# A fused decoder layer on one core: the rows of the last stage turned by the DMA queue in place of TensorE

## The reference

```python
x = x + attn(layernorm(x), ...)                    # 32 query heads, int4 codes with scales
x = x + xattn(layernorm(x), ctx, ...)              # q1 @ q2, both fake-quantised to 0..255
x = x + einsum('bsi,oi->bso', layernorm(x), bw)    # bw: binarised weight, 1024 x 1024

def fake_quant(x, scale, zp):
    q = clip(round(x / scale + zp), 0, 255)
    return (q - zp) * scale
```

## Time and profile before

| | us |
|---|---|
| median of 3 runs | 1130.78 (1128.71 to 1130.89) |
| the profiled execution's own time | 1129.51 |
| its span, first to last instruction | 1127.6 |
| PE busy | 1067.3 (95%) |
| DVE busy | 933.2 (83%) |
| ACT busy | 697.0 (62%) |
| mean granted clock of TensorE | 0.99 |

### The profile page before, as it was taken

One profiled execution on the slowest core, in us unless ns is written; L12 is line 12 of the kernel. 1 busy time (PEld: TensorE's weight loads), 2 busy tenths in 40 slices (PEclk: granted clock), 3 DMA queues, 4 the chain that ended last, 5 costly groups with the idle time before them and its releaser, 6 DMA issues.

```text
span 1127.6 us, 19107 instructions
## 1 busy us (share of the span) xinstructions
PE 1067.3 (95%) x5544; PEld 524.7 (47%) x5544; DVE 933.2 (83%) x1760; ACT 697.0 (62%) x1509; POOL 693.5 (62%) x771
## 2 busy tenths in 40 slices
PE   3898998899999999999999999999999998889997
PEld 2443444344444444444444444454454454444553
DVE  6878787789888888888888889999999988867663
ACT  4356564766777777777777776666666666443320
POOL 2457445887776776776776777877787777232100
PEclk8899999999999999999999999999999999999999
DMA  9343221577777767667657756777767755501111
GB/s 353 110 150 113 66 99 38 120 157 151 167 142 158 159 138 158 159 137 158 161 134 155 163 135 143 156 153 155 165 144 148 159 120 117 180 1 38 38 37 39
DMA packets 280915, 148.66 MB, mean 132 GB/s; under 512 B 228976, under 2 KB 241520, under 8 KB 280848
## 3 DMA queue, kind: packets, MB, share of 16 engines
q1 hardware_dynamic: 273072, 134.47, 51.4%
q10 hardware_dynamic: 7776, 13.37, 4.2%
HBM read 89.07 MB, written 4.19 MB: 83 GB/s over the span
## 4 chain that ended last, share of the span: by engine, by line
PE 79%; DVE 6%; ACT 6%; issue 5%; POOL 2%; ACTq 1%; DMA 1%; SPq 0%; DVEq 0%; POOLq 0%
PE side_ps L642 9%; PE side_ps L644 9%; PE side_ps L643 9%; PE side_ps L787 9%; PE out_ps L807 8%; PE proj_ps L807 8%; PE proj_ps L642 4%; PE proj_ps L644 4%; PE proj_ps L643 4%; PE score_ps L770 3%; PE score_ps L772 2%; PE score_ps L771 2%; PE out_ps L662 2%; PE score_ps L662 2%; PE score_ps L915 2%
## 5 line engine op out<-in xcount | busy, mean ns | idle before, releaser
L1418 POOL TENSOR_TENSOR w_b<-prob,w_b 128x896 f16<-128x896 f32 (+2 forms) x192 | 188.9, 999 | 28.6 <-ACT w_b L1118 28.1
L642 PE MATMUL side_ps<-hT,w_a 128*128 128x512 f16 x504 | 191.1, 379 | 1.5 <-DVE rot L1778 1.5
L644 PE MATMUL side_ps<-hT,w_a 128*128 128x512 f16 x504 | 191.0, 379 | 0.0
L643 PE MATMUL side_ps<-hT,w_a 128*128 128x512 f16 x504 | 191.0, 379 | 0.0
L1873 DVE SCALAR_TENSOR_TENSOR x_acc<-proj_ps,o_now,x_acc 128x1024 f32<-128x1024 f32 x120 | 153.5, 1279 | 38.2 <-PE proj_ps L807 38.2
L1411 POOL TENSOR_SCALAR prob<-prob,row_inv 128x512 f32<-128x512 f32 (+3 forms) x256 | 170.7, 682 | 22.7 <-DVE row_inv L1946 16.9
L1091 ACT ACTIVATE prob<-score_ps,neg_max 128x512 f32<-128x512 f32 (+3 forms) x256 | 132.9, 521 | 47.7 <-DVE neg_max L1849 38.8
L1425 POOL TENSOR_TENSOR q_sb<-rot,q_sb 128x512 f16<-128x512 f32 x64 | 75.2, 1176 | 139.1 <-ACT q_sb L1083 139.1
L1873 DVE SCALAR_TENSOR_TENSOR x_acc<-out_ps,o_now,x_acc 128x1024 f32<-128x1024 f32 x120 | 152.7, 1272 | 1.3 <-PE out_ps L807 1.3
L807 PE MATMUL proj_ps<-work,w_b 128*128 128x512 f16 x496 | 127.3, 379 | 2.0 <-issue 1.1
L807 PE MATMUL out_ps<-work,w_b 128*128 128x512 f16 x496 | 127.3, 379 | 1.7 <-DVE x_acc L1873 1.7
(11 more groups left out here) (224 smaller groups left out, 2151.2 us busy)
## 6 DMA issues: line engine op xcount, KB each, us to landing
stage_c<-in_codes_dram SPq DMA_DIRECT2D x80, 256.0 KB, 2.9
stage_o<-in_codes_dram SPq DMA_DIRECT2D x64, 256.0 KB, 3.9
stage_s<-in_scales_dram SPq DMA_DIRECT2D x64, 256.0 KB, 3.8
ctx_raw<-in_ctx_dram ACTq DMA_DIRECT2D x32, 256.0 KB, 3.3
x_acc<-in_x_dram SPq DMA_DIRECT2D x8, 512.0 KB, 8.3
k_sb<-in_codes_dram SPq DMA_DIRECT2D x16, 256.0 KB, 6.2
v_sb<-in_scales_dram SPq DMA_DIRECT2D x16, 256.0 KB, 6.9
x_acc<-in_ffn_w_dram ACTq DMA_DIRECT2D x16, 256.0 KB, 2.6
```

The source lines that it names most:

```text
L642: pe.matmul(o, stat(0), mov(0), start=first, stop=False)
L643: pe.matmul(o, stat(0), mov(1), start=False, stop=False)
L644: return pe.matmul(o, stat(1), mov(0), start=False, stop=last)
L1418: ins = pool.tensor_tensor(prob16[:, 1, to:to + w], prob[:, at:at + w], prob16[:, 0, to:to + w], ALU.subtract)
```

## The change

For tiles 2 to 7 TensorE no longer turns `h3`. ACT's new `h3_high(t)` writes the upper f16 half of the unturned rows to `h3_halves[:, 0]` in SBUF, in two pieces of 512, DVE's new `h3_low(t)` the lower half to `h3_halves[:, 1]` in one piece of 1024, and SP's `h3_by_queue(t)` turns the three pieces by DMA into `h3_T`. For tiles 3 to 7 TensorE no longer turns `i1`, and ACT no longer copies it: `i1_by_queue(t)` turns the row of codes by DMA. `dense(t)` for t of 2 and more takes the 16 products with the upper half first and the 8 with the lower half behind them; their number is as before. On DVE `h3_low(t)` stands between `y_part(t - 1, 0)` and `y_part(t - 1, 1)`, where `h3_lo(t)` stood behind both. On ACT `h3_high(t)` stands ahead of `x1_scale(t + 2)`, where `h3_part(t)` stood behind `x1_round(t + 2)`. The arithmetic is the same.

```diff
+H3_BY_PE = 2
+I1_BY_PE = 3
...
+        h3_halves = w_b[:, 1, 2 * D:4 * D].rearrange("p (l n) -> p l n", l=2)
...
@@ SP
-            for t in range(TT):
+            def store(t):
                 sp.wait_ge(y_ready, 2 * t + 2)
                 sp.dma_start(out_rows[t].rearrange("p (k t) -> p k t", t=P), x1_rows(t)).then_inc(out_stored, 16)
+            def i1_by_queue(t):
+                sp.wait_ge(xat_done, 2 * (t - 2) + 2)
+                sp.wait_ge(i1_ready, t + 1)
+                sp.dma_start_transpose(i1_T[:, t % 2, :, :], i1[:, t % 2, :]).then_inc(i1_by_dma[t % 2], 16)
+            def h3_by_queue(t):
+                sp.wait_ge(ffn_done, 2 * (t - 2) + 2)
+                for u in range(2):
+                    sp.wait_ge(h3_upper, 2 * (t - H3_BY_PE) + u + 1)
+                    sp.dma_start_transpose(h3_T[:, t % 2, 0, 4 * u:4 * u + 4, :], h3_halves[:, 0, u * S:(u + 1) * S])\
+                        .then_inc(h3_up_turned[t % 2][u], 16)
+                sp.wait_ge(h3_lower, t - H3_BY_PE + 1)
+                sp.dma_start_transpose(h3_T[:, t % 2, 1, :, :], h3_halves[:, 1, :]).then_inc(h3_low_turned[t % 2], 16)
+            store(0)
+            i1_by_queue(I1_BY_PE)
+            for t in range(H3_BY_PE, TT):
+                h3_by_queue(t)
+                store(t - 1)
+                if t + 2 < TT:
+                    i1_by_queue(t + 2)
+            store(TT - 1)
@@ PE, cross
-                pe.wait_ge(i1T_ready, t + 1)
+                if t < I1_BY_PE:
+                    pe.wait_ge(i1T_ready, t + 1)
+                else:
+                    pe.wait_ge(i1_by_dma[t % 2], 16 * ((t - I1_BY_PE) // 2 + 1))
@@ PE, dense
+                    if t >= H3_BY_PE:
+                        for k in range(KB):
+                            if h == 0 and k % 4 == 0:
+                                pe.wait_ge(h3_up_turned[t % 2][k // 4], 16 * ((t - H3_BY_PE) // 2 + 1))
+                            for l in range(2):
+                                pe.matmul(proj_ps[:, h, :], h3_T[:, t % 2, 0, k, :],
+                                          bw_pair(k // 2, l)[:, k % 2, h * S:(h + 1) * S], start=(k, l) == (0, 0), stop=False)
+                        if h == 0:
+                            pe.wait_ge(h3_low_turned[t % 2], 16 * ((t - H3_BY_PE) // 2 + 1))
+                        for k in range(KB):
+                            mm = pe.matmul(proj_ps[:, h, :], h3_T[:, t % 2, 1, k, :],
+                                           bw_pair(k // 2, 0)[:, k % 2, h * S:(h + 1) * S], start=False, stop=k == KB - 1)
+                        mm.then_inc(ffn_done, 1)
+                        continue
...
-                    if t and h == 0 and t + 2 < TT:
-                        turn_i1(t + 2)
...
-                turn_h3(t)
+                if t < H3_BY_PE:
+                    turn_h3(t)
@@ ACT
+            def h3_high(t):
+                act.wait_ge(h3_ready, t + 1)
+                for u in range(2):
+                    if t > H3_BY_PE:
+                        act.wait_ge(h3_up_turned[(t - 1) % 2][u], 16 * ((t - 1 - H3_BY_PE) // 2 + 1))
+                    act.activation(h3_halves[:, 0, u * S:(u + 1) * S], h3[t % 2][:, u * S:(u + 1) * S], ACT.Copy, scale=H_UP)\
+                        .then_inc(h3_upper, 1)
...
-                if 0 < t < TT - 1:
+                if 0 < t < I1_BY_PE - 1:
                     i1_T_part(t + 1)
                 if t:
                     next_roots(2 if more else 1)
+                if t >= H3_BY_PE:
+                    h3_high(t)
...
-                if t:
+                if 0 < t < H3_BY_PE:
                     h3_part(t)
@@ DVE
+            def h3_low(t):
+                dve.wait_ge(h3_upper, 2 * (t - H3_BY_PE) + 2)
+                if t > H3_BY_PE:
+                    dve.wait_ge(h3_low_turned[(t - 1) % 2], 16 * ((t - 1 - H3_BY_PE) // 2 + 1))
+                dve.scalar_tensor_tensor(h3_halves[:, 1, :], h3[t % 2], H_UP, h3_halves[:, 0, :],
+                                         ALU.mult, ALU.subtract).then_inc(h3_lower, 1)
...
                     y_part(t - 1, 0)
+                if t >= H3_BY_PE:
+                    h3_low(t)
                 if t:
                     y_part(t - 1, 1)
+                if 0 < t < H3_BY_PE:
                     h3_lo(t)
```

More of the change, by code:

```diff
@@ L450, in build @@
         h3_split = sem("h3_split")
+        h3_upper = sem("h3_upper")
+        h3_lower = sem("h3_lower")
+        h3_up_turned = [[sem(f"h3_up_turned{r}_{u}") for u in range(2)] for r in range(2)]
+        h3_low_turned = [sem(f"h3_low_turned{r}") for r in range(2)]
+        i1_by_dma = [sem(f"i1_by_dma{r}") for r in range(2)]
         ffn_done = sem("ffn_done")
@@ L1329, in x1_sum @@
                     act.wait_ge(prob_turned, TURNED * N_SLOTS)
-                if t >= 2:
+                if t >= 2 + I1_BY_PE:
+                    act.wait_ge(i1_by_dma[t % 2], 16 * ((t - 2 - I1_BY_PE) // 2 + 1))
+                elif t >= 2:
                     act.wait_ge(i1_turned, t - 1)
```

## The result

| | before | changed |
|---|---|---|
| median us | 1130.52 (5 runs) | 1122.46 (5 runs, 1120.11 to 1123.64) |
| profiled execution, its span | 1129.51, 1127.6 | 1122.46, 1120.5 |

The ratio is 0.9931, with a 95% interval of 0.9916 to 0.9946. The forecast was 1122.2 us.

A forecast was written before the change was run, and what follows sets the result against it. TensorE, without a gap, was taken as the bound; 4.35 us (f32 transposes), 2.25 (codes) and 2.10 (tile 7) sum to 8.70 off the median 1130.78, giving 1122.08, stated as 1122.2 us; 8-in-10 range 1120.0 to 1125.5.

The forecast's parts named there:

- What bounds the stage: Last stage: TensorE, busy for all of each 15.13 us period, sets it; removing its transposes and tile 7's gap saves 8.70 us.
- The new order of the products: Dense products, upper half first: priced at nothing; if weight-load cover went, 0.094 us more per product, 4.5 us a tile.
- The chain: Loop through DVE, ACT and queue from dense product start S: row ready S + 7.49, transpose issued S + 8.17, wanted S + 13.81.
- the root's wait: DVE's wait for ACT's square root in the normalised row: falls from 1.32 us to 0.27 as ACT's copy goes.
- the room: Time from first upper piece's issue to TensorE wanting it: 5.64 us at tiles 3 to 5, 6.93 at 6, 3.48 at 7.
- the slower rival: Queue's latency sets the period, S + 8.17 + L with landing time L; at 8.0 us 4 us slower, 1134.8; chance 0.03.
- The landings: Queue transposes of 4 and 8 blocks: 3.0 us from issue to landing, bounds 2.3 and 6.2.
- A late last tile: Rival at tile 7: one of its three transfers takes long and PE waits as before; 1124.2 us, chance 0.14.
- the rival ahead of it: Every tile waits a little: landings above 5.64 us cost tiles 3 to 5 the excess each; 1126.5 us, chance 0.04.

The follow-up runs named there:

- old_order: Changed kernel with the lower half's product of each block put back behind the two of the upper half: 1123.29 us, ratio 0.9935.
- spare2: Changed kernel with two spare one-block transposes issued ahead of each tile's first upper piece: 1124.53 us, ratio 0.9955.
- spare4: Changed kernel with four spare one-block transposes issued ahead of each tile's first upper piece: 1133.96 us, ratio 1.0045.
- spare4_two: Changed kernel with four spare transposes at tiles 3 and 4 only: 117.25 us from tile 0's first dense product to y's last half (changed kernel 113.30).
- h3_i1_from_1: Changed kernel with tile 1's normalised rows and tile 2's codes also turned by the queue: 1121.2 us, ratio 0.9933; once more, 1119.36 us.
- h3_from_1: Changed kernel with tile 1's normalised rows also turned by the queue: 1118.38 us, ratio 0.9904.

## Why the prediction was right

**What bounds the stage.** Right. 5 x 0.87 and 5 x 0.45 us left PE's list, the 2.10 us ahead of tile 7 went with its transposes, and all came off the stage one for one, singly (6.47, 2.24) and together (8.71). The new order of the products left their 0.216 us alone. The nearness of the number owes something to chance. 1122.2 was forecast and 1122.46 measured, but the five executions lie between 1120.11 and 1123.64, and the profiled one took 1122.46 where 1120.81 was worked out, by the later start. What fits closely is the stage, 8.71 for 8.70.

**The chain.** Right for tiles 3 to 7: at tile 5 7.29 us measured for 7.29, the root's wait 0.27, the room 5.56 to 5.58 for 5.64 at tiles 3 to 5, 6.87 for 6.93 at tile 6, 3.42 for 3.48 at tile 7. Wrong at tile 2. It was given more than 5.64 us, and the changed trace has 1035.20 (issue) to 1039.76 (wanted), 4.56. The reason given was PE's wait for the split of tile 1's turned rows. But that split is DVE's own work, and tile 2's residual stands behind it in DVE's list:

```profile
1025.11 1.29 DVE L2081 SCALAR_TENSOR_TENSOR w_b<-out_ps,w_b 128x512 f16<-128x512 f32 x2 [2.82 <-ACT w_b L1411]
...
1027.17 0.74 DVE L2066 SCALAR_TENSOR_TENSOR swapped<-score_ps,sums,w_a 128x512 f32<-128x512 f32 x1
```

Tile 1's dense product starts at 1025.95, so the second residual half comes 1.22 us behind it in place of 0.20, and 5.58 less 1.02 is the 4.56. The formula of the slower rival leaves tile 2 out for the same reason. That cost nothing at landings of 2.5 us; old_order and spare2 lost at tile 2 by it.

**The landings.** 3.0 was taken, from 5 and 7 blocks. Measured 2.4 to 2.5 for 4 blocks, and 3.1 to 4.4 for 8. So the last tile had 0.9 us to spare, not half a microsecond. The codes behind a store took up to 4.8 and had over 9 us. The estimate by the Trainium skill (DMA: Bandwidth & Descriptors, "Anatomy of one DMA"), whose fit is for another issuing engine, was 2.3 and 2.6; the shorter agrees within 0.2, the 8 blocks took 0.5 more at the least, and the measurement decides.

**The rivals.** A late last tile did not come about. The run of transposes one after another cost 1.16 there, not 2.0, since a piece took 2.5 us. The slower rival's formula failed, and with it the price per tile of the rival ahead of it, which uses the same loop. "The same loop, now S + 8.17 + L, is the period" takes the chain to start with the dense product; it starts with the end of the cross product, and in spare4 tiles 3 and 5 started on time at a delay that by the formula costs each tile 1.9. The sign held (ratio 1.0045), the price per tile didn't. Where the formula's total fitted, in spare4_two, it did so by a slow stretch of PE, and in spare4 such a stretch brought it nearer.

## What to carry to other kernels

Where one engine has no gap, take work off its list and count it in full; then count for every tile, the first and the last by themselves, when the new route's data are wanted and when they can land. Draw such a loop from the instruction that really releases the chain: work issued ahead of a wait isn't held up by it, so late data can cost every second tile. And when a total fits a theory, look at whether the waits stand where the theory has them.

## What the hardware showed

- A transpose of 4 blocks of 128x128 from SBUF to SBUF landed 2.4 to 2.5 us after its issue, one of 8 blocks 3.1 at the least; they were issued 1.25 us apart and were under way side by side. In the changed kernel a DMA share of 0.5 beside the products cost them nothing.
- The granted clock of TensorE after an idle stretch of some 2 us is not the same each time. It fell to 0.60 behind 2.02 us in one trace (h3_i1_from_1) and to 0.67 behind 2.10 in another (spare4_two), and stayed at 1.00 behind 2.03 in a third and behind 2.96 and 1.95 in spare4, where behind the wait of 4.05 it fell to 0.60 for 3.7 us. Where it fell, some 1.7 us were lost with PE shown as busy. What decides it is open.
- h3_from_1 is faster than the kernel before by 0.96% (ratio 0.9904); the changed kernel's ratio is 0.9931, taken on another occasion. By the stage the difference is 2.28 us.
